# Four value-spread transfers started at separate points of a group, their mask in four instructions, and the key spread as one product

## The chip, the cores and the metric

One Trainium2 chip, and one of its cores. The metric is the device time of one launch in microseconds (us), of the slowest core; here there is only one. Five engines work beside each other: TensorE (matrix products; PE in the profile, PEld its weight loads), VectorE (DVE), ScalarE (ACT), GpSimd (POOL) and SyncE (SP), which starts most DMA transfers. They order their work by semaphores.

## The reference, cut to what matters

The program is a two-layer block: an attention layer, an expert layer (best two of eight), a second attention of another kind, an expert layer (best one), each followed by a sum and a layer norm. The change touches only the first attention. Its core, for 4096 tokens (16 sequences of 256), 128 channels in 16 heads of 8:

```
cs = cumsum(w, time);  cs_b = cs - w          # w: learned decay, per channel
A_f = (r * exp(cf)) @ (k * exp(-cf)).T        # cf, cb: cs and cs_b, shifted and clipped
A_b = (r * exp(-cb)) @ (k * exp(cb)).T
A   = where(i >= j, A_f, A_b)                 # per head, 256 x 256
y   = A @ v
```

Then y is normalized over each head, gated, projected, added to x and normalized; the rows go on to their experts.

## The kernel before, in words

`lion_stage` (from L130) computes this attention in eight groups n = 0 to 7 of 512 tokens. A head has only 8 channels, so TensorE works on four heads at once: keys are spread into a tile `kx` in which each of four copies keeps the channels of one head of four and holds zeros elsewhere, and values into a tile `vx`, of which likewise only the channels of a head are kept. Scores of one group are computed in eight parts m = 0 to 7 (`scores`, L432); each part's scores go from PSUM to SBUF by a ScalarE copy (L688), VectorE puts the other triangle in place (L895), and TensorE multiplies with the values (`attend`, L452), one part behind. Between these, each engine's `step(n)` does pieces of the projection work for group n+1 and of the closing work for group n-1, in an order written out by hand.

Scores of part m increase `s_sc` to 8n+m+1, so `s_sc >= 8(n-1)+5` says that part 4 of group n-1 is done.

The path of the values: in part 3 of group n-1 ScalarE writes the projected values of group n to `vt` (L643). SyncE (`spread_values`, L290) stores them in HBM (L294, 256 KB) and, when that has landed, reads them back in another order by four transfers, one for each 32 partitions of `vx` (L299, 256 KB each, all with the same source). GpSimd multiplies `vx` with the 0/1 matrix `vhead` (`mask_values`, L596, the instruction L600, 128x2048). `attend(n, 0)` waits for it, in part 1 of group n. SyncE's list continues with the residual rows (L315), the input of group n+3 (L273, after part 6 of group n) and the store of the finished rows (L303).

GpSimd's list in each group n: the scatter of group n-2's rows to the experts' regions (L573, eight indirect DMAs; not in groups 0 and 1), the mask for group n+1, the norm of group n-1 (L580 to L593). A scatter waits for VectorE's `dispatch` (L877) in part 3.

The keys: VectorE spreads one half (`spread`, L752; L755, four instructions of 128x256) of `kx` and ScalarE the other (L627), each in two halves of a group: half 0 for group n+1 in part 6, half 1 in part 3. After half 0 VectorE does, in part 7, the gate (L790) and the mix input of group n+2 (L763, L764, L765), for which TensorE waits in part 0 (L345).

Of the kernel before, what the change touches and what calls it, by code (L numbers as in the profile page):

```python
# [18 lines left out]
ALU = mybir.AluOpType  # L19
# [3 lines left out]
P = 128  # L23
# [3 lines left out]
GT = 4  # L27
GTOK = GT * P
# [101 lines left out]
def lion_stage(nc, sem, x_in, x_out, w, consts, route):  # L130
# [15 lines left out]
    with ctx:  # L146
        def sb(name, shape, dt=F32):
            return ctx.enter_context(nc.sbuf_tensor("a_" + name, shape, dt))
# [5 lines left out]
        C = {k: con[:, a:b] for k, (a, b) in where.items()}  # L154
# [27 lines left out]
        rk = [sb(f"rk{i}", [P, 4, GTOK]) for i in range(2)]  # L182

        kx = sb("kx", [P, 2, GTOK // 32, 4, 32])
        vx = [sb(f"vx{i}", [P, GTOK // 32, P]) for i in range(2)]
# [65 lines left out]
        s_vd, s_vxp, s_vx = [[sem(f"lion_v_{n}_{i}") for i in range(2)] for n in ("stored", "spread")] + [sem("lion_v_chunks")]  # L251
        s_kk, s_kd, s_ktp, s_kt = sem("lion_keys_scaled"), sem("lion_r_scaled"), sem("lion_keys_transposed"), sem("lion_key_rows")
        s_kx = sem("lion_keys_spread")
        s_stp, s_st = sem("lion_states"), sem("lion_states_masked")
        s_sc, s_ata, s_atd = sem("lion_scores"), sem("lion_scores_copied"), sem("lion_diagonals_masked")
# [14 lines left out]
        @block.sync  # L270
        def _(sp):
            one = lambda rows, n: rows[n]
            load_x = lambda n: sp.dma_start(xp[n % 2][:, :, 1:SEQ + 1], xT_rows[n]).then_inc(s_x[n % 2], 16)  # L273
            sp.wait_ge(s_zero, 4)
            load_x(0)
            loads = [(con[:], consts[:, columns]), (maa[:], w["maa"]), (maa_w1[:], w["maa_w1"]),
                     (dec_w1[:], w["dec_w1"]), (dec_w2[:], w["dec_w2"]), (decay[:], w["decay"]),
                     (wT[:], w["wT"]), (woe[:, 0:P], w["wT"][:, 4, :]), (lnwb[:], w["lnwb"]), (gw[:], route["gate_w"])]
            for dst, src in loads:
                sp.dma_start(dst, src).then_inc(s_w, 16)  # L280
            for f in range(NF):
                r = D_MIX * (f % 4)
                sp.dma_start(maa_w2[r:r + D_MIX, f // 4, :], w["maa_w2"][f]).then_inc(s_w, 16)
            load_x(1)
            for b in range(2):
                sp.dma_start(xr[b][:], x_rows[b]).then_inc(s_xr[b], 16)
            sp.wait_ge(s_padr, 1)
            sp.dma_start(route["regions"][DUMMY * P:DUMMY * P + P], pad[:]).then_inc(s_pads, 16)

            def spread_values(n):  # L290

                b = n % 2
                sp.wait_ge(s_vt, n + 1)
                sp.dma_start(v_rows[b], vt[:]).then_inc(s_vd[b], 16)  # L294
                if n >= 2:
                    sp.wait_ge(s_y, n - 1)
                sp.wait_ge(s_vd[b], 16 * (n // 2) + 16)
                for h in range(4):
                    sp.dma_start(vx[b][32 * h:32 * h + 32], v_chunks[b]).then_inc(s_vxp[b], 16)  # L299

            def store_rows(n):
                sp.wait_ge(s_xo, n + 1)
                sp.dma_start(o_rows[n], xo[n % 2][0][:, :, 0:P]).then_inc(s_out[n % 2], 16)  # L303

            spread_values(0)
            for n in range(NG):
                if n + 1 < NG:
                    spread_values(n + 1)
                if n == 0:
                    sp.wait_ge(s_xf, NF)  # L310
                    sp.wait_ge(s_xgp, 1)
                    load_x(2)
                if n and n + 1 < NG:
                    sp.wait_ge(s_z, n)
                    sp.dma_start(xr[(n + 1) % 2][:], x_rows[n + 1]).then_inc(s_xr[(n + 1) % 2], 16)  # L315
                if n + 3 < NG:
                    sp.wait_ge(s_sc, 8 * n + 7)
                    load_x(n + 3)
                if n:
                    store_rows(n - 1)  # L320
                if n == NG - 3:
                    for dst, src in route["weights"]:
                        sp.dma_start(dst, src).then_inc(s_mw, 16)
            store_rows(NG - 1)
            sp.wait_ge(s_tab, 1)
            for e in range(NE):
                end = sp.value_load(ends[0:1, e:e + 1], min_val=0, max_val=e * REGION + TOK)
                sp.dma_start(route["regions"][bass.ds(end, P), :], pad[:]).then_inc(s_pads, 16)
            for b in range(2):
                sp.wait_ge(s_out[b], 16 * (NG // 2))  # L330
            sp.wait_ge(s_mw, 16 * len(route["weights"]))
            sp.wait_ge(s_pads, 16 * (1 + NE))
# [216 lines left out]
        def _(pool):  # L549
# [46 lines left out]
            def mask_values(n):  # L596

                b = n % 2
                pool.wait_ge(s_vxp[b], 64 * (n // 2) + 64)
                nc.gpsimd.tensor_tensor(vx[b][:], vx[b][:], C["vhead"].unsqueeze(1).broadcast_to([P, GTOK // 32, P]),  # L600
                                        ALU.mult).then_inc(s_vx, 1)

            pool.wait_ge(s_w, NW)
            mask_values(0)
            for n in range(NG):
                if n >= 2:
                    scatter(n - 2)
                if n + 1 < NG:
                    mask_values(n + 1)
                if n:  # L610
                    norm(n - 1)
# [128 lines left out]
        def _(dve):  # L740
            v = nc.vector
# [9 lines left out]

            def spread(n, half):  # L752

                for h in range(4):
                    i = v.tensor_scalar(kx[:, 0, 8 * half:8 * half + 8, h, :],  # L755
                                        rk[n % 2][:, 1, half * 256:half * 256 + 256].rearrange("p (c j) -> p c j", j=32),
                                        C["heads4"][:, h:h + 1], None, ALU.mult)
                i.then_inc(s_kx, 1)

            def mix_input(k):  # L760
                b = k % 2
# [189 lines left out]
            scale_r(0)  # L951
            dve.wait_ge(s_kk, 1)
            spread(0, 0)
            gate(0)
            mix_input(1)
# [1746 lines left out]
```

## Time and profile before

| | us |
|---|---|
| three runs | 1222.15, 1222.37, 1225.36 (median 1222.37) |
| profiled execution, its own time | 1220.72 |
| its span | 1218.6 |
| TensorE busy (matmul) | 959.9 (79%) |
| VectorE busy | 749.2 (61%) |
| ScalarE busy | 554.4 (45%) |
| GpSimd busy | 487.4 (40%) |

The span reaches from the first to the last instruction of the profiled execution; 2.1 us lie around it. Matmul ends are modelled, so a busy TensorE isn't one at its peak. The stage with the change fills about the first 396 us. A row of the timeline gives start, duration, engine, line, operation, output tile and inputs, and shape, with how many instructions were merged; the bracket gives the idle time before it and what ended it. "issue" there means that nothing which the profile shows was waited for, and "remote" that the releaser wasn't identified.

### The profile page before, as it was taken

To read this page: it belongs to the slowest core of one execution; us is meant where nothing else is said; L and a number is where in the kernel's file an instruction comes from. 1 tells how busy PE (TensorE), PEld (TensorE's weight loads), DVE (VectorE), ACT (ScalarE), POOL (GpSimd) and SP (SyncE) were. 2 spreads that over 40 slices of the span, in tenths; PEclk is the share of its full clock that TensorE was granted. 3 is DMA by queue.
4 is the path that set the end of the run, shared out by engine and by line. 5 is a ranking of instruction groups with operands and counts; after the bars stand their busy time and mean duration, and the time that the engine had idled before them with its cause. 6 is when DMAs were issued, how large, how long until landed. Compare 5 with 4: busy or idle time off the path is not lost. (4 is left out here: it accounts for less than half of the span.)

```text
span 1218.6 us, 34137 instructions
## 1 busy us (share of the span) xinstructions
PE 959.9 (79%) x12733; PEld 678.2 (56%) x12734; DVE 749.2 (61%) x2236; ACT 554.4 (45%) x1120; POOL 487.4 (40%) x596
## 2 busy tenths in 40 slices
PE   5689898889871699995488858569999998525995
PEld 2456565556560688895244436466566664214885
DVE  3768786777544355553288875914887655742664
ACT  1365555456520355552266752144444444314664
POOL 0113334532546244443477620021164332533776
PEclk8798998898855799998699998867977666757998
DMA  3122321325201222220433331131111124002210
GB/s 92 37 63 70 74 54 51 89 71 175 71 29 52 59 56 58 58 56 25 115 87 88 62 87 65 70 89 61 47 54 54 54 60 160 18 13 54 56 53 22
DMA packets 122117, 79.50 MB, mean 65 GB/s; under 512 B 46979, under 2 KB 108521, under 8 KB 121600
## 3 DMA queue, kind: packets, MB, share of 16 engines
q1 hardware_dynamic: 115328, 64.95, 19.9%
q0 software_dynamic: 6656, 12.70, 3.3%
q8 instruction: 93, 1.52, 0.5%
q14 instruction: 40, 0.33, 0.1%
HBM read 49.05 MB, written 27.51 MB: 63 GB/s over the span
## 5 line engine op out<-in xcount | busy, mean ns | idle before, releaser
L1134 ACT ACTIVATE bx_h<-bx_up,bx_cur 128x128 f32<-128x128 f32 x288 | 82.1, 368 | 104.2 <-PE bx_up L1105 104.2
L573 POOL DMA_INDIRECT regions_b<-a_xo,a_seat x64 | 63.6, 994 | 149.7 <-DVE a_seat L877 132.6
L688 ACT ACTIVATE a_at<-a_scores 128x1024 f32<-128x1024 f32 x64 | 65.5, 1024 | 120.2 <-PE a_scores L447 89.9
L1063 POOL DMA_INDIRECT chosen_b<-bx_ys,bx_to x72 | 76.4, 1061 | 90.4 <-DVE bx_ys L1177 88.5
L442 PE MATMUL a_scores<-a_rk,a_kx 32*128 32x128 f32 (+3 forms) x1024 | 72.8, 317 | 27.3 <-issue 11.5
L442 PEld LDWEIGHTS a_scores<-a_rk,a_kx 32*128 32x128 f32 x1024 | 55.5, 210 | 55.6 <-issue 38.6
L1105 PE MATMUL bx_up<-bx_xT,bx_cur 128*128 128x128 f32 x576 | 82.8, 288 | 1.9 <-issue 0.5
L1087 PE MATMUL bx_down<-bk_w,bx_h 128*128 x576 | 82.0, 285 | 0.4 <-ACT bx_h L1134 0.4
L1105 PEld LDWEIGHTS bx_up<-bx_xT,bx_cur 128*128 128x128 f32 x576 | 71.4, 195 | 11.1 <-issue 5.3
L600 POOL TENSOR_TENSOR a_vx<-a_vx,a_con 128x2048 f32<-128x2048 f32 x8 | 36.2, 4525 | 99.0 <-DMA a_vx<-lion_values 99.0
L1087 PEld LDWEIGHTS bx_down<-bk_w,bx_h 128*128 128x128 f32 x576 | 69.8, 191 | 3.9 <-issue 0.6
L1331 PE MATMUL c_bank<-c_xT,c_wc 128*128 128x512 f32 x128 | 60.6, 616 | 11.1 <-ACT c_xT L1450 11.1
L1150 DVE TENSOR_SCALAR bx_cur<-bk_w 128x516 f32 x72 | 30.9, 429 | 58.5 <-issue 55.8
L447 PE MATMUL a_scores<-a_rk,a_kx 32*128 32x32 f32 (+3 forms) x1024 | 64.9, 301 | 0.9 <-issue 0.8
L2152 POOL COPY g_kak<-keep_k 128x512 f32<-128x512 f32 x16 | 13.6, 857 | 101.6 <-POOLq L2654 76.9
L447 PEld LDWEIGHTS a_scores<-a_rk,a_kx 32*128 32x128 f32 x1024 | 53.5, 216 | 1.0 <-issue 0.8
L1985 PE MATMUL g_hidden<-g_xT,g_g 128*128 128x512 f32 x64 | 49.2, 869 | 3.4 <-ACT g_hid L2287 3.4
L1402 POOL TENSOR_SCALAR c_xn<-c_part,c_mv,c_rsv 128x128 f32<-128x128 f32 x32 | 35.0, 1104 | 37.8 <-ACT c_rsv L1444 37.8
L1331 PEld LDWEIGHTS c_bank<-c_xT,c_wc 128*128 128x128 f32 x128 | 24.5, 196 | 45.2 <-issue 43.1
L2387 DVE TENSOR_TENSOR g_xyx<-g_eye,g_wu_xy 128x256 f32<-128x256 f32 x12 | 5.0, 421 | 71.7 <-PE g_wu_xy L1945 71.7
L895 DVE COPY_PREDICATED a_at<-a_earlier,a_scores 128x256 f32<-128x256 uint32 x64 | 28.1, 439 | 32.6 <-ACT a_at L688 31.6
L1105 PE MATMUL dx_up<-dx_xT,dx_cur 128*128 128x128 f32 x320 | 47.1, 291 | 0.7 <-ACT dx_cur L1123 0.2
(431 smaller groups left out, 2564.2 us busy)
## 6 DMA issues: line engine op xcount, KB each, us to landing
a_vx<-lion_values SPq DMA_DIRECT2D x32, 256.0 KB
bx_xs<-regions_b SPq DMA_DIRECT2D x72, 65.0 KB, 1.8
bk_w<-in_b_w SPq DMA_DIRECT2D x16, 256.0 KB, 5.9
c_part<-chosen_b SPq DMA_DIRECT2D x16, 256.0 KB, 3.9
space<-in_d_w SPq DMA_DIRECT2D x16, 256.0 KB
dx_xs<-regions_d SPq DMA_DIRECT2D x40, 65.0 KB, 1.8
a_xp<-in_a_xT SPq DMA_DIRECT2D x8, 256.0 KB, 3.4
a_xr<-in_x SPq DMA_DIRECT2D x8, 256.0 KB
```

The lines of the kernel that those rows point to most:

```text
L442: mm(S4[:, g, o:o + P - 32 * q], kx[rows, 0, 4 * t + q].rearrange("p h j -> p (h j)"), rk[b][rows, 0, t * P + 32 * q:(t + 1) * P], start=T ...
L447: i = mm(S4[:, g, o + P - 32 * q:o + P + 32], kx[rows, 1, 4 * t + q].rearrange("p h j -> p (h j)"), rk[b][rows, 2, t * P:t * P + 32 * q + 32],
L573: nc.gpsimd.indirect_dma_start(route["regions"], bass.IndirectOffsetOnAxis(ap=seat[b][:, k, t:t + 1], axis=0), xo[b][k][:, t, :], None).th ...
L600: nc.gpsimd.tensor_tensor(vx[b][:], vx[b][:], C["vhead"].unsqueeze(1).broadcast_to([P, GTOK // 32, P]), ALU.mult).then_inc(s_vx, 1)
L688: op(at[m % 2][:], S4[:, :, 0:320].rearrange("p g (q k) -> p g q k", q=2)[:, :, :, 0:P], ACT.Copy).then_inc(s_ata, 1)
L1063: nc.gpsimd.indirect_dma_start(dest, bass.IndirectOffsetOnAxis(ap=to[u][:, 0:1], axis=0), ys[u][:], None, bounds_check=dest.shape[0] - 1, ...
L1087: i = mm(BY[u % 2][:, 0:P], h[u % 2][:, f, :], w2[:, bass.ds(e, 1), f, :].rearrange("p e c -> p (e c)"), start=(f == 0), stop=(f == FC - 1))
L1105: i = mm(BU[u % 2][:, f * P:(f + 1) * P], cur[u % 2][:, f * P:(f + 1) * P], xT[u % 2][:], start=True, stop=True)
L1134: i = op(h[u % 2][:, f, :], BU[u % 2][:, f * P:(f + 1) * P], act_fn, bias=cur[u % 2][:, FC * P + f:FC * P + f + 1])
L1331: i = mm(B[1 + k].rearrange("p (s t) -> p s t", s=GSEQ), wc[:, k, j, :], xT[:, :, j:SEQ + j], start=(j == 0), stop=(j == 3))
L1402: nc.gpsimd.tensor_scalar(xn[:, t, :], part[b][0][:, t, :], mv[:, t, 0:1], rsv[:, t:t + 1], ALU.subtract, ALU.mult).then_inc(s_xn, 1)
L1985: mm(H[j % 2].rearrange("p (k h c) -> p k h c", h=4, c=32), g1[:], x.unsqueeze(2).broadcast_to([P, 4, 4, 32]), start=True, stop=False)
```

## The change

SyncE starts the first of the four transfers as before; the others wait until parts 4, 5 and 6 of the group before have their scores (from the second group on). GpSimd's mask is written as four instructions of 128x512, with the semaphore on the last. VectorE's half of the key spread is one product of 128x1024, with the keys and the 0/1 columns both broadcast, in place of four instructions that scale by a column. What is computed stays the same.

```diff
                 for h in range(4):
+                    if n and h:
+                        sp.wait_ge(s_sc, 8 * (n - 1) + 4 + h)
                     sp.dma_start(vx[b][32 * h:32 * h + 32], v_chunks[b]).then_inc(s_vxp[b], 16)
...
-                nc.gpsimd.tensor_tensor(vx[b][:], vx[b][:], C["vhead"].unsqueeze(1).broadcast_to([P, GTOK // 32, P]),
-                                        ALU.mult).then_inc(s_vx, 1)
+                for t in range(GT):
+                    i = nc.gpsimd.tensor_tensor(vx[b][:, 4 * t:4 * t + 4], vx[b][:, 4 * t:4 * t + 4],
+                                                C["vhead"].unsqueeze(1).broadcast_to([P, 4, P]), ALU.mult)
+                i.then_inc(s_vx, 1)
...
-                for h in range(4):
-                    i = v.tensor_scalar(kx[:, 0, 8 * half:8 * half + 8, h, :],
-                                        rk[n % 2][:, 1, half * 256:half * 256 + 256].rearrange("p (c j) -> p c j", j=32),
-                                        C["heads4"][:, h:h + 1], None, ALU.mult)
-                i.then_inc(s_kx, 1)
+                keys = rk[n % 2][:, 1, half * 256:half * 256 + 256].rearrange("p (c j) -> p c j", j=32)
+                v.tensor_tensor(kx[:, 0, 8 * half:8 * half + 8], keys.unsqueeze(2).broadcast_to([P, 8, 4, 32]),
+                                C["heads4"].unsqueeze(1).unsqueeze(3).broadcast_to([P, 8, 4, 32]), ALU.mult).then_inc(s_kx, 1)
```

## Rows read from the trace of the kernel before

**Rows 1.** The page's first line: span and instructions.
```profile
span 1218.6 us, 34137 instructions
```

**Rows 2.** Stretches (length; busy PE, PEld, DVE, ACT, POOL; clock; DMA; GB/s).
```profile
187.00:228.00 41.00, 36.21 (x557) 23.93 (x556) 29.68 (x91) 22.26 (x32) 17.43 (x17) 0.92 0.25 66
...
188.00:190.00 2.00, 1.03 (x3) 0.85 (x3) 0.00 (x0) 0.00 (x0) 1.98 (x2) 0.50 0.66 195
...
289.00:291.00 2.00, 2.00 (x28) 0.97 (x22) 0.77 (x3) 1.97 (x3) 0.00 (x0) 1.00 1.03 366
```

**Rows 3.** ScalarE's timeline: copies of part 6, group 1; parts 5, 6, group 3.
```profile
109.35 1.02 ACT L688 ACTIVATE a_at<-a_scores 128x1024 f32<-128x1024 f32 x1 [1.08 <-PE a_scores L447]
...
183.13 1.02 ACT L688 ACTIVATE a_at<-a_scores 128x1024 f32<-128x1024 f32 x1 [4.21 <-remote]
...
192.29 1.02 ACT L688 ACTIVATE a_at<-a_scores 128x1024 f32<-128x1024 f32 x1 [6.25 <-PE a_scores L447]
```

**Rows 4.** TensorE's timeline, part 6 of group 3 and part 0 of group 4.
```profile
188.84 2.02 PE L442 MATMUL a_scores<-a_rk,a_kx 32*128 32x128 f32 x5 [0.95 <-issue]
...
200.85 1.12 PE L345 MATMUL a_free<-a_xin,a_maa_w 128*128 128x512 f32 x2 [0.22 <-DVE a_xin L765]
```

**Rows 5.** GpSimd's timeline: first scatter, mask, norm, copy of rows, group 3.
```profile
178.84 1.12 POOL L573 DMA_INDIRECT regions_b<-a_xo,a_seat  x1 [19.66 <-DVE a_seat L877]
...
188.81 4.54 POOL L600 TENSOR_TENSOR a_vx<-a_vx,a_con 128x2048 f32<-128x2048 f32 x1
...
193.65 1.04 POOL L583 TENSOR_TENSOR a_rsv<-a_vr,a_power 128x4 f32<-128x4 f32 x1
...
198.13 0.61 POOL L593 COPY a_xo<-a_xo 128x512 f32<-128x512 f32 x1
```

**Rows 6.** Timeline of group 7: scores of part 5, their copy, scores of part 6.
```profile
345.22 0.79 PE L447 MATMUL a_scores<-a_rk,a_kx 32*128 32x128 f32 x8
...
347.88 1.02 ACT L688 ACTIVATE a_at<-a_scores 128x1024 f32<-128x1024 f32 x1 [5.94 <-remote]
...
353.58 0.58 PE L442 MATMUL a_scores<-a_rk,a_kx 32*128 32x96 f32 x4 [0.89 <-issue]
```

**Rows 7.** SyncE's timeline, group 3: store, four spread transfers, residual load.
```profile
175.77 0.37 SPq L294 DMA_DIRECT2D lion_values<-a_vt  x1
178.12 2.05 SPq L299 DMA_DIRECT2D a_vx<-lion_values  x4
186.91 0.39 SPq L315 DMA_DIRECT2D a_xr<-in_x  x1
```

**Rows 8.** VectorE's timeline: mix input without overlap, then from the key spread, group 3.
```profile
78.51 0.68 DVE L763 TENSOR_TENSOR a_nb<-a_xp 128x512 f32<-128x512 f32 x1
...
195.10 1.21 DVE L755 TENSOR_SCALAR a_kx<-a_rk,a_con 128x256 f32<-128x256 f32 x4
197.33 0.45 DVE L895 COPY_PREDICATED a_at<-a_earlier,a_scores 128x256 f32<-128x256 uint32 x1 [1.02 <-ACT a_at L688]
...
198.43 0.86 DVE L763 TENSOR_TENSOR a_nb<-a_xp 128x512 f32<-128x512 f32 x1
...
201.65 0.18 DVE L843 TENSOR_TENSOR a_lg<-a_mv,a_gsum 128x32 f32<-128x32 f32 x1
```

**Rows 9.** Timeline: key spreads that a mask overlaps (start-up, groups 0, 1).
```profile
37.58 5.41 DVE L755 TENSOR_SCALAR a_kx<-a_rk,a_con 128x256 f32<-128x256 f32 x4
38.09 4.49 POOL L600 TENSOR_TENSOR a_vx<-a_vx,a_con 128x2048 f32<-128x2048 f32 x1 [36.48 <-DMA a_vx<-lion_values]
...
43.14 0.81 PE L442 MATMUL a_scores<-a_rk,a_kx 32*128 32x128 f32 x8 [5.50 <-DVE a_kx L755]
...
73.65 4.01 DVE L755 TENSOR_SCALAR a_kx<-a_rk,a_con 128x256 f32<-128x256 f32 x4
...
112.17 2.89 DVE L755 TENSOR_SCALAR a_kx<-a_rk,a_con 128x256 f32<-128x256 f32 x4
```

**Rows 10.** Grouped instructions of the stretch 0 to 400 us: the key spread.
```profile
L755 DVE TENSOR_SCALAR a_kx<-a_rk,a_con 128x256 f32<-128x256 f32 x64 | 27.8, 494 | 0.0
```

## The prediction

> **What bounds the kernel now.** The change lies in the first of five stages, so I read that stage alone; of the profile's page I use only the span [rows 1], since its chain of waits follows the last stage. The stage runs eight groups of 512 tokens, each in parts 0 to 7. First view: busy times by stretch. In one group period of 41 us TensorE is busy 36.2, VectorE 29.7, GpSimd 17.4 [rows 2]: TensorE leads, and what makes it wait costs whole time. Second view: ScalarE's timeline. Its copy of part 5's scores comes at 183.13 and of part 6's at 192.29, 9.2 us apart, the latter after a wait of 6.25 for TensorE [rows 3]. TensorE in turn shows one or two matmuls at a time with gaps that no wait explains ("issue") [rows 4], busy 1.03 of 2 us, and the granted clock falls to 0.50, the 1.2 GHz level [rows 2]. This stall recurs in groups 2 to 6. It lies over GpSimd's eight indirect DMAs (the scatter, 178.84 to 188.8) [rows 5].
>
> Is it the spread's burst (four transfers begun within 2.05 us from 178.12 [rows 7]) or the scatter? Three readings speak. Group 1 has the burst and no scatter: there the copy of part 6 waits only 1.08 us [rows 3]. Group 7 has a scatter and no burst: ScalarE's copy of part 5 still starts at 347.88, though the scores it reads ended at 346.0, and TensorE shows the same "issue" gaps until 353.58 [rows 6]. And while weights stream in at 366 GB/s TensorE is busy 2.00 of 2 us [rows 2]. So the scatter makes most of the stall. From these rows the stall of a middle group is about 7.4 us (2.6 on ScalarE, 183.13 less 180.5 where the scores ended by the pattern of group 7; 4.8 on TensorE), that of group 7 4.6 (1.9, and 2.7 of gaps): at most 2.8 us can belong to burst and other transfers.
>
> **The change, part by part.** All sums are against the profiled execution, 1220.7 us (span 1218.6 and 2.1 around it); the median of the runs is 1.7 above it, so I add the sum to 1222.4.
>
> (1) Three extra waits on SyncE. The spread for group n+1 is begun in part 4 of group n, after its store: store at 175.77, spread at 178.12 [rows 7]. Transfer 1 waits for part 4's scores (done at 176.6): nothing changes. Transfer 2 waits for part 5's, done about 180.5, so it moves by 1.4 us, and only transfer 3 really moves, to the end of part 6's scores: 192.3. So three of the four still run under the scatter. Behind that wait on SyncE stand the load of the residual (now 186.91 [rows 7]), the next input load and the store of rows. The first is used more than a group later, the second by a mix step a group later, the third is waited for two groups later: all hidden, and cost would begin only beyond some 30 us of lateness. What it relieves: the last transfer and the residual load no longer run beside the scatter. Bounds per group: 0, and the 2.0 us by which the copy of part 6 (192.29) lies after the stall's end at about 190.3 [rows 3, 4]; I take 0.5, nearer to 0, since group 7 stalls with neither, for the four groups 3 to 6: -2.0 us.
>
> (2) The mask comes later. It needs all four landed. Before, it starts at 188.81, directly behind the scatter [rows 5], and ends at 193.3, where VectorE has nothing to do. Now the last transfer starts at 192.35; the store of the same 256 KB takes 2.35 us from issue to the next step [rows 7], so the mask starts near 194.8 and, 4.5 us long, runs under VectorE's spread of keys (195.10) and mix input (198.43 to 200.8) [rows 8]. What the trace shows of the two beside each other: a key spread in the old form takes 5.41, 4.01 and 2.89 us where a mask overlaps it, 1.21 where none does [rows 8, 9]. For an operation with two inputs in SBUF there is one sort of row: L763 takes 0.86 us when a GpSimd copy from 198.13 to 198.74 overlaps its start, 0.68 when none does [rows 5, 8]: it waited almost until the copy's end.
>
> The Trainium skill says the same on the page "SBUF — State Buffer", section "Who interferes with whom": a VectorE instruction with two SBUF inputs contends with a GpSimd instruction that reads SBUF, and whichever starts first blocks the other for its whole length. It speaks against the new form of the key spread as an escape from the port. The trace agrees as far as the 0.86 against 0.68 goes; by the rule with whole pieces of 1.13 us the two waits worked out below would come to +2.1 us a group in place of 1.5, and without any contention to 0.
>
> With the mask in four instructions a piece takes 4.53/4 = 1.13 us, and one waits up to 1.0, typically 0.85 of it. Order in a middle group: piece 1 from 194.85; the key spread waits 0.75 (hidden: VectorE is idle 1.02 us before its next step, at 197.33 [rows 8]); piece 2 after it; piece 3 ahead of L763; piece 4 between L763 and L764. Two waits of 0.85, less the 0.2 which L763 loses already: +1.5 us. It is on the path, for TensorE waits 0.22 us for exactly this mix input at 200.85 [rows 4]. Bounds: 0 (VectorE always wins, or no contention) and 3.0 (three waits of 1.0). Group 6 has no mix input after it, so groups 2 to 5 pay: +6.0.
>
> Queued behind the mask on GpSimd: the norm's small operations (193.65, 1.04 us [rows 5]) move from 193.3 to about 201; VectorE reads their result at 201.65 [rows 8], itself moved to 203: hidden by about 1 us. Scatter and dispatch come 15 us later, and TensorE needs the masked values only about 10 us after the mask.
>
> (3) Three places where the old long mask blocks a key spread. Start-up: 5.41 instead of 1.2 us, and TensorE waits 5.50 us for it until 43.14 [rows 9]. Now the spread (37.58) is issued ahead of the mask (38.09) and runs free: 4.2 us gained, less two piece waits (1.7) in the mix input which TensorE wants next: -2.5, bounds -4.2 and 0. Group 0: 4.01-1.21 = 2.8 gained, 0.9 for a piece that the key spread waits for and 1.7 in the mix input lost: -0.2. Group 1: 2.89-1.21 = 1.7 gained, 2.6 lost: +0.9. Bounds for each of these two: the gain alone, and the loss with three full waits.
>
> (4) One product in place of four. Operations of this kind take 0.18 us for 32 columns and 0.68 for 512 [rows 8], so 1.05 ns a column and 1.22 us for 1024, against a mean of 4 x 0.344 that in fact overlap to 1.14: +0.09 us each. (The mean of 494 ns in the grouped row contains the blocked ones [rows 10].) Sixteen of them; the eight of part 6 lie in the 1.02 us of slack, those of part 3 are waited for by TensorE: 8 x 0.09 = +0.7. Bounds -0.5 and +3.
>
> Four mask instructions instead of one add perhaps 0.1 us each on GpSimd, inside the hidden part.
>
> Sum: -2.0 +6.0 -2.5 -0.2 +0.9 +0.7 = +2.9. Forecast: 1222.4+2.9 = **1225.3 us**, own range 1219 to 1230: a small loss that a measurement (0.3%, 3.7 us) hardly separates from none.
>
> **Rivals.**
> A, the mix input isn't held up: VectorE wins each tie, or isn't held by the pieces at all. Then part 2 is 0, start-up gives -4.2, groups 0 and 1 -2.8 and -1.7, part 4 +0.7, relief -2: -10, 1212. For it: ties of a few tenths decide. Against: the 0.86.
> B, the burst is the stall's main cause. Spacing takes half of 7.4 us in five groups (-18) while the mask still costs +5: 1209; if all of it goes, 1190. For it: burst and scatter begin within 1 us of each other. Against: group 7, and the burst is three quarters unmoved.
> C, slower: the later mask meets VectorE in full. Mechanism: each of the mix input's three operations waits a whole piece (3.0 in groups 2 to 5, 12 us), and the norm, a further 2 us late on GpSimd, makes VectorE's expert choice wait 0.5 us five times (2.5); start-up gains only 1.4, groups 0 and 1 lose 3, part 4 0.7, no relief: +17, 1239; with half of this 1231. It decides once the last transfer lands over 2.5 us after part 6, so that more pieces lie behind 198.4.
> That the waits change nothing (all met when reached) holds for the first of them, and is excluded for the third, since SyncE is there 12 us before part 6 ends.
>
> **How the numbers follow.** Forecast 0.45, A 0.22, B 0.08, C 0.25. Range 1209 to 1236: it takes in A, B's half, and C to above its half; what is left out is B's full case and C's full price, under 2 in 10. Within 0.3% means 1218.7 to 1226.0. Of the forecast's 0.45, 0.27 lies within and 0.18 above; A gives 0.20 faster, 0.02 same; B 0.08 faster; C 0.23 slower, 0.02 same. Faster 0.28, same 0.31, slower 0.41.
>
> **What would show it.** In the new profile: SyncE's fourth issue right behind part 6's scores; the mask's first piece 2.4 us later, and pieces with VectorE's L763 to L765 operations between them, each with a longer duration (about 1.5) than now; the "issue" gaps of TensorE still there in groups 2 to 6 until the scatter ends; start-up's key spread at 1.2 us and TensorE's first scores near 39. I am wrong if the gaps shrink by more than 2 us a group (B), if L763 to L765 keep 0.7 us beside a mask piece (A), or if the mask's end delays the norm past VectorE's choice (C).

## The result, and the profile after

The changed kernel takes 1241.93 us (median; 1238.38 to 1251.3), the kernel before in the same comparison 1223.86: a ratio of 1.0129, 95% interval 1.0081 to 1.0176. So it is slower, by 16 us at this ratio where 2.9 were forecast, and outside the range. The page's first line answers to [rows 1]:
```profile
span 1241.8 us, 34113 instructions
```
The span is 23.2 us longer. The first stage ends (first load of the next stage) at 421.73 us in place of 401.77: 20.0 of these lie in it, and 2.3 of these had passed before any changed instruction ran (the first store, 31.05 against 28.78).

First view, ScalarE's timeline of the changed kernel: the copies of the scores, which mark each part. The lines are those of [rows 3] (part 6 of group 1; parts 5 and 6 of group 3), with part 7 of group 3 and parts 0 and 1 of group 4 behind them.
```profile
114.14 1.02 ACT L692 ACTIVATE a_at<-a_scores 128x1024 f32<-128x1024 f32 x1 [1.08 <-PE a_scores L449]
...
194.08 1.02 ACT L692 ACTIVATE a_at<-a_scores 128x1024 f32<-128x1024 f32 x1 [4.20 <-remote]
...
203.02 1.02 ACT L692 ACTIVATE a_at<-a_scores 128x1024 f32<-128x1024 f32 x1 [6.03 <-PE a_scores L449]
...
207.23 1.02 ACT L692 ACTIVATE a_at<-a_scores 128x1024 f32<-128x1024 f32 x1 [1.59 <-PE a_scores L449]
...
209.97 1.02 ACT L692 ACTIVATE a_at<-a_scores 128x1024 f32<-128x1024 f32 x1 [0.60 <-PE a_scores L449]
...
216.99 1.02 ACT L692 ACTIVATE a_at<-a_scores 128x1024 f32<-128x1024 f32 x1
```
From part 5 to part 6 are 8.94 us, 9.16 before [rows 3]: the stall is untouched. From part 0 to part 1 are 7.02, where the kernel before has 5.10:
```profile
199.02 1.02 ACT L688 ACTIVATE a_at<-a_scores 128x1024 f32<-128x1024 f32 x1 [0.59 <-PE a_scores L447]
...
204.12 1.02 ACT L688 ACTIVATE a_at<-a_scores 128x1024 f32<-128x1024 f32 x1
```
This last step is longer in each group but the last: by 3.0, 3.0 and 3.3 us at start-up and in groups 1 and 2, by 1.5 to 2.2 in groups 3 to 6, in sum 16.7 us. (Steps are named by the group whose scores are copied; the prediction's middle "groups 2 to 5" begin the masks of groups 3 to 6.)

Second view, the timelines of SyncE, GpSimd, VectorE and TensorE in the same place; they answer to [rows 7], [rows 5], [rows 8] and [rows 4].
```profile
189.00 14.32 SPq L301 DMA_DIRECT2D a_vx<-lion_values  x4
...
206.10 6.23 POOL L603 TENSOR_TENSOR a_vx<-a_vx,a_con 128x512 f32<-128x512 f32 x4 [6.33 <-DMA a_vx<-lion_values]
...
209.38 1.83 DVE L765 TENSOR_TENSOR a_nb<-a_xp 128x512 f32<-128x512 f32 x1
...
211.24 1.64 DVE L766 SCALAR_TENSOR_TENSOR a_dx<-a_nb,a_xp 128x512 f32<-128x512 f32 x1
...
212.91 0.75 DVE L767 SCALAR_TENSOR_TENSOR a_xin<-a_dx,a_maa,a_xp 128x512 f32<-128x512 f32 x1
...
213.72 0.70 PE L347 MATMUL a_free<-a_xin,a_maa_w 128*128 128x512 f32 x1 [2.13 <-DVE a_xin L767]
```
The four issues now span 14.32 us in place of 2.05; the mask begins 2.8 us after the last one's issue is done (203.3), 6.3 us after GpSimd was free for it. Its four pieces take 6.23 us in place of 4.53, because VectorE's operations come between them; L765 and L766 take 1.83 and 1.64 us in place of 0.86 and about 0.7, and TensorE waits 2.13 us for the mix input, 0.22 before.

Third view, a stretch of 2 us under the scatter, which answers to the second line of [rows 2].
```profile
198.00:200.00 2.00, 0.85 (x4) 0.50 (x4) 0.00 (x0) 0.00 (x0) 1.46 (x2) 0.81 0.10 33
```
Four matmuls in 2 us, VectorE and ScalarE idle, as before; DMA is busy 0.10 of this stretch where it was 0.66 before. With hardly a transfer beside it the stall goes on, though three of the four transfers still ran under its beginning.

### The profile page after: what moved, and what is told of

It reads as the page before. It is cut to its first block and busy times, and to the rows that moved or that the text cites. A ratio compares the mean times of both kernels' runs of the same rounds, so it can differ in the third digit from the quotient of the medians.

```text
span 1241.8 us, 34113 instructions
## 1 busy us (share of the span) xinstructions
PE 985.9 (79%) x12733; PEld 688.0 (55%) x12734; DVE 758.9 (61%) x2188; ACT 554.4 (45%) x1120; POOL 504.5 (41%) x620
## 5 line engine op out<-in xcount | busy, mean ns | idle before, releaser
L603 POOL TENSOR_TENSOR a_vx<-a_vx,a_con 128x512 f32<-128x512 f32 x32 | 48.3, 1538 | 135.6 <-DMA a_vx<-lion_values 135.6
L444 PE MATMUL a_scores<-a_rk,a_kx 32*128 32x128 f32 (+3 forms) x1024 | 73.2, 321 | 19.1 <-issue 11.2
L1333 PE MATMUL c_bank<-c_xT,c_wc 128*128 128x512 f32 x128 | 63.6, 643 | 9.2 <-ACT c_xT L1452 9.1
```

Source lines behind the costliest of these rows:

```text
L444: mm(S4[:, g, o:o + P - 32 * q], kx[rows, 0, 4 * t + q].rearrange("p h j -> p (h j)"), rk[b][rows, 0, t * P + 32 * q:(t + 1) * P], start=T ...
L603: i = nc.gpsimd.tensor_tensor(vx[b][:, 4 * t:4 * t + 4], vx[b][:, 4 * t:4 * t + 4], C["vhead"].unsqueeze(1).broadcast_to([P, 4, P]), ALU.mult)
L1333: i = mm(B[1 + k].rearrange("p (s t) -> p s t", s=GSEQ), wc[:, k, j, :], xT[:, :, j:SEQ + j], start=(j == 0), stop=(j == 3))
```

## The experiments

The runs were made on five chips, and that turned out to matter, so each group names its chip. "The waits" are the change's on SyncE, "four pieces" its mask, "one product" its key spread. All ratios are against the kernel before on the same chip.

**Chip 1, the kernel before at 1224.6 us: the change taken apart.** My first theory was that the waits bring the late mask, and with it the whole loss; the rival, that the new key spread or the pieces cost by themselves.

The waits alone:
```
 for h in range(4):
+    if n and h:
+        sp.wait_ge(s_sc, 8 * (n - 1) + 4 + h)
```


> The kernel before with the three added waits of the transfers alone; mask and key spread as before. Theory (the late mask under VectorE's work is the price): the 4.5 us mask now starts near the key spread of part 6, which waits for nearly all of it, 3 to 4 us less the 1 us of slack in each of groups 1 to 6, so slower by 12 to 20 us. Rival 1 (the other two edits make the loss): no slower than 2 us. Rival 2 (the spacing relieves TensorE's gaps under the scatter): gaps shrink by over 2 us a group.

Measured 1.0162 (1.0115 to 1.0210). The waits alone lose all of it, as much as the whole change within the intervals. VectorE and GpSimd, group 3:
```profile
207.06 5.39 DVE L757 TENSOR_SCALAR a_kx<-a_rk,a_con 128x256 f32<-128x256 f32 x4
...
207.69 4.61 POOL L602 TENSOR_TENSOR a_vx<-a_vx,a_con 128x2048 f32<-128x2048 f32 x1 [6.81 <-DMA a_vx<-lion_values]
```
Late, the long mask meets the key spread (5.39 us in place of 1.21 [rows 8]), and the mix input begins 6.24 us after the key spread does (213.30), 3.33 before [rows 8].

The mask in four instructions alone:
```
-nc.gpsimd.tensor_tensor(vx[b][:], vx[b][:], ...)
+for t in range(GT):
+    i = nc.gpsimd.tensor_tensor(vx[b][:, 4 * t:4 * t + 4], ...)
```


> The kernel before with the mask in four instructions alone. Theory: in groups 2 to 6 the mask stays where VectorE is idle, so nothing; in start-up and groups 0 and 1 a key spread of four instructions waits for pieces and not for a whole mask, but mix input meets the rest: between -4 and +1 us. Rival (four pieces cost by themselves): slower by over 3 us.

Measured 1.0009 (0.9973 to 1.0044): nothing.

One product alone (the diff's last part):
```
-for h in range(4):
-    i = v.tensor_scalar(kx[:, 0, 8 * half:8 * half + 8, h, :], ...)
+v.tensor_tensor(kx[:, 0, 8 * half:8 * half + 8], keys..., heads4..., ALU.mult)
```


> The kernel before with the key spread as one product alone. Theory: 0.09 us longer at 8 places on the path and still blocked by the long mask in start-up and groups 0 and 1: between -1 and +2 us. Rival (the product is what costs): slower by over 4 us.

Measured 1.0019 (0.9981 to 1.0057). The start-up shows why there is no gain:
```profile
37.90 1.21 DVE L755 TENSOR_TENSOR a_kx<-a_rk,a_con 128x1024 f32<-128x1024 f32 x1
...
38.13 5.36 POOL L600 TENSOR_TENSOR a_vx<-a_vx,a_con 128x2048 f32<-128x2048 f32 x1 [36.52 <-DMA a_vx<-lion_values]
...
39.64 4.41 DVE L761 TENSOR_TENSOR a_nb<-a_xp 128x512 f32<-128x512 f32 x1
...
45.62 2.07 PE L345 MATMUL a_free<-a_xin,a_maa_w 128*128 128x512 f32 x2 [2.37 <-DVE a_xin L763]
```
The key spread, begun 0.23 us ahead of the mask, takes 1.21 us in place of 5.41 [rows 9], and now it is the mask that takes longer (5.36 us for 4.49). The mix input's first operation waits instead (4.41 for 0.68). The wait is moved on. Not every operation of VectorE waits: between the two the gate (L788), which reads one of its inputs from PSUM, starts at 39.04 under the mask and takes its usual 0.69 us.

Four pieces and one product, without the waits:

> Both of these, without the waits. Theory: the whole loss of the change hangs on the waits, so this is within -4 and +2 us of the kernel before. Rival: it keeps a third or more of the 16 us loss.

Measured 0.9986 (0.9945 to 1.0026). With waits_only it shows that on this chip the loss hangs on the waits.

**Chip 0, the kernel before at 1215.7 us: when the mask runs.**

Four pieces, one product, no waits on SyncE, but GpSimd waits until VectorE has scaled the queries in part 6, the step just ahead of the key spread, which was meant to start the mask as late as the change does:
```
+if n:
+    pool.wait_ge(s_kd, n + 1)
 for t in range(GT):
```


> The changed kernel without the waits on the transfers; in their place GpSimd itself waits, before each mask from group 1 on, until VectorE has scaled part 6's queries (about when the last transfer lands in the changed kernel). Theory (the mask's place is the price, however it comes there): as slow as the changed kernel, 1.0 to 1.6% above the kernel before. Rival (the transfers' own spacing or their meeting with other loads is the price): within 0.4% of the kernel before.

Measured 0.9908 (0.9874 to 0.9942): faster, against my theory. But the theory was hardly tried: only the masks begun in groups 0 and 1 were held back by the new wait; from group 2 on it was met when GpSimd reached it, and the mask began directly behind the scatter (in group 3 the scatter's last DMA ends at 190.70, the mask begins at 190.72).

The changed kernel, the mask held back until the mix input is done:
```
+if n + 1 < NG:
+    pool.wait_ge(s_xin, n + 2)
```


> The changed kernel, with GpSimd waiting before each mask until VectorE's mix input has been written, so that the two no longer run side by side. The mask comes 2 to 3 us later still. Theory (contention with the mix input is the price): its three operations take 0.7 us each and the kernel gains 6 to 14 us on the changed one, unless the norm behind the mask is then late for VectorE's choice of experts (up to 2 us a group given back). Rival (lateness itself is the price): slower than the changed kernel.

Measured 0.9975 (0.9953 to 0.9996). The changed kernel itself didn't run on this chip; why holding the mask back gains so little is shown by the repeat on chip 3, below.

The changed kernel, its last transfer begun with the third, at the scores of part 5:
```
-sp.wait_ge(s_sc, 8 * (n - 1) + 4 + h)
+sp.wait_ge(s_sc, 8 * (n - 1) + (5, 6, 6)[h - 1])
```


> The changed kernel with the last transfer waiting for part 5's scores in place of part 6's, so that it lands while the scatter still runs. Theory: the mask is back behind the scatter in groups 2 to 6 and the loss is gone but for groups 0 and 1: within 0.4% of the kernel before. Rival (any spacing costs): slower by over 0.7%.

Measured 0.9874 (0.9837 to 0.9912).

The kernel before, the spread of groups 2 to 7 cut to a sixteenth:
```
-sp.dma_start(vx[b][32 * h:32 * h + 32], v_chunks[b])
+sp.dma_start(vx[b][32 * h:32 * h + 32, 0:1], v_chunks[b][:, 0:1])
```


> The kernel before, but from group 2 on each of the four transfers moves one sixteenth of its data (the values of these groups are left stale): what the burst itself costs. Theory (the scatter makes the gaps of TensorE, not the burst): gaps under the scatter stay, at most 2 us a group shorter, so 0 to 8 us faster. Rival (the burst makes them): the copy of part 6 follows that of part 5 by 4 us in place of 9.2, and the kernel is over 20 us faster.

Measured 0.9992 (0.9959 to 1.0024). All four profiles surprised me in one thing: part 4 to 5 takes 3.88 us and 5 to 6 some 4.8 in groups 3 to 6, together 8.7, where each profile so far had about 6.5 and 9, together 15.2 to 15.7. The stall was gone from kernels that share no edit. Either each takes it away by its own doing, or it hangs on the chip.

**Chip 6, the kernel before at 1229.6 us: two of them again, beside both kernels.**

> The kernel before, unchanged, profiled once more. Open is why the four last profiles (mask_late_by_wait, mask_after_mix, last_at_part5, small_spread) show no stall under the scatter: their copies of the scores of part 5 and part 6 start 3.9 and 4.8 us after the copy ahead of them, where every earlier profile has 6.5 and 9.1. Theory S: the stall is a state of the chip or of the execution, and no edit took it away. Then this profile can show either pattern, and it shows the one that the other three profiles of this call show; without the stall the scatter ends before the group does, and the long mask meets the key spread, so that from the copy of part 7 to that of part 0 there are about 8.2 us in place of 2.7, group period about 40, and the span stays within 10 us of 1218. Theory T: each of the four edits takes the stall away by its own doing. Then this profile shows 6.5 and 9.1 again (period 41), whatever the others show.

> The changed kernel, unchanged, profiled once more beside before_again. Theory S: it has or lacks the stall as before_again does. With the stall the ratio is 1.013 again (1.008 to 1.018). Without it, the last transfer waits for the scores of part 6, which now come 7 us earlier, the mask still runs under the mix input (part 0 to part 1 about 9.4 us), but the key spread is no longer held: period about 37.5 to 38.5 against 40, so a ratio of about 0.985 to 0.995: the sign of the change would turn with the stall. Theory T: ratio 1.013 and steps of 6.5 and 9.1.

> last_at_part5 once more (the changed kernel, its last transfer begun at the scores of part 5 as the third is). Theory S: it shows the stall if before_again does, and then costs about 1.005 to 1.013 of before, like the changed kernel; without the stall 0.987 again. Theory T: no stall (3.9 and 4.8 us) and 0.987 in either case, while before_again has the stall.

> mask_late_by_wait once more (the kernel before, GpSimd waiting for VectorE's key spread of part 6 ahead of the mask; nothing of the change). Theory S: as before_again: with the stall about 1.01 (the one long mask under the mix input, what the late mask costs by itself), without it 0.991 again. Theory T: no stall and 0.991 whatever before_again shows.

(The text on record errs in one point: mask_late_by_wait holds the four pieces and the one product too, as shown above; it lacks only the waits on SyncE.) All four profiles have the stall: together 15.7 to 15.8 us in groups 3 to 6. Ratios: before_again 1.0005 (0.9968 to 1.0043), after_again 1.0078 (1.0043 to 1.0114), last_again 1.0005 (0.9962 to 1.0049), mask_late_again 1.0127 (1.0083 to 1.0171). The same two kernels that gained 0.9 and 1.3% on chip 0 lose 1.3% or gain nothing here. The stall belongs to the chip, not to an edit. (Each chip appears in one group of runs only, so chip and hour can't be told apart.)

mask_late_again is also the run that shows the cause. It has no wait on SyncE; here GpSimd's own wait does hold the mask back, by 6.61 us in group 3,
```profile
201.64 6.24 POOL L603 TENSOR_TENSOR a_vx<-a_vx,a_con 128x512 f32<-128x512 f32 x4 [6.61 <-DVE a_rk L804]
```
and it loses at least as much as the change beside it (three executions). last_again, whose mask begins directly behind the scatter (186.79 in group 3), loses nothing. So the lateness of the mask is the price, and not the spacing of the transfers.

**Chip 3, the kernel before at 1214.7 us.**

The changed kernel with `range(GT)` of the mask's loop cut to `range(1)`:

> The changed kernel with only the first of the four mask instructions (three quarters of the spread values stay unmasked). Transfers and waits stay those of the change. Theory M: the loss is the late mask beside VectorE's mix input and key spreads. Then L765 and L766 of the mix input fall from 1.8 and 1.6 to 0.7 us, the step from part 0 to part 1 from 6.9 to about 5, and the ratio from 1.008 to 1.013 down to 0.990 to 0.998 (the four-piece mask with the one product and no waits gave 0.9986 with the pieces still there). Theory Q: the three waits cost by themselves, through what is queued behind them on SyncE or through later transfers. Then the ratio stays at 1.005 or above though the mix input is short.

Measured 0.9611 (0.9547 to 0.9676), the stage ending at 347.9 us. VectorE and TensorE, group 3 to 4:
```profile
172.69 0.70 DVE L765 TENSOR_TENSOR a_nb<-a_xp 128x512 f32<-128x512 f32 x1
...
173.43 0.69 DVE L766 SCALAR_TENSOR_TENSOR a_dx<-a_nb,a_xp 128x512 f32<-128x512 f32 x1
...
174.15 0.75 DVE L767 SCALAR_TENSOR_TENSOR a_xin<-a_dx,a_maa,a_xp 128x512 f32<-128x512 f32 x1
...
174.96 1.12 PE L347 MATMUL a_free<-a_xin,a_maa_w 128*128 128x512 f32 x2
```
With all three waits in place, each operation is back at its undisturbed time and TensorE waits for nothing. The gain is larger than theory M gave (0.990 to 0.998), which was worked out for a chip with the stall; it also leaves out three quarters of the mask's own time on GpSimd. Theory Q finds no support, but this chip could hardly show it, for here the waits hold the mask back by 0.43 us at most from group 2 on; what speaks against Q is mask_late_again.

Two repeats, wanted on a chip with the stall; this one has none, so they only repeat chip 0:

> mask_after_mix once more (the changed kernel, GpSimd waiting for the mix input ahead of the mask), wanted on a chip that shows the stall. Theory M as a pure port cost: the step from part 0 to part 1 is back to about 5 us and the ratio near 0.998. Theory M with the queue: the norm is queued behind the mask on GpSimd, so VectorE's expert choice (L847) waits about 5 us for a_rsv, the step from part 1 to part 2 grows from 4.7 to about 10, and the ratio is 1.01 or more with the stall, against 0.9975 on the chip without it.

> small_spread once more (the kernel before, the spread of groups 2 to 7 cut to a sixteenth of its bytes, old values kept), wanted on a chip that shows the stall. If the spread's burst makes half of the stall or more (rival B of the prediction), the steps part 4 to 5 and 5 to 6 fall below 5.2 and 7.0 us and the ratio below 0.99. If the burst has no part in it, they stay at 6.5 and 9.1 and the ratio is 0.997 to 1.003. If this chip has no stall at all, before_again on another chip doesn't tell, and the ratio is 0.999 as it was.

Measured 1.0000 (0.9970 to 1.0029) and 0.9979 (0.9947 to 1.0010). Both kernels of small_spread leave most of the values out. Whether that would shorten the stall on a chip that has it stays untried. mask_after_mix_again shows what queues behind a held mask (GpSimd, then VectorE's expert choice):
```profile
199.89 4.93 POOL L605 TENSOR_TENSOR a_vx<-a_vx,a_con 128x512 f32<-128x512 f32 x4 [4.67 <-DVE a_xin L769]
...
205.12 1.05 POOL L585 TENSOR_TENSOR a_rsv<-a_vr,a_power 128x4 f32<-128x4 f32 x1
...
206.20 0.19 DVE L847 TENSOR_TENSOR a_lg<-a_mv,a_gsum 128x32 f32<-128x32 f32 x1 [5.53 <-POOL a_rsv L585]
```
The mix input is free (0.68, 0.69, 0.75 us) and the norm pays: the step from part 1 to 2 is 10.5 us in place of 4.7.

The kernel before with GpSimd's order turned:
```
-scatter(n - 2); mask_values(n + 1); norm(n - 1)
+mask_values(n + 1); norm(n - 1); scatter(n - 2)
```


> The kernel before with another order on GpSimd: mask, norm, and only then the scatter of the group before. If the scatter's eight indirect DMAs bring the stall, it leaves parts 4 to 6 (steps 3.9 and 4.8 us in groups 2 to 6) and stands where the scatter now runs, under parts 0 to 3 of the next group, with TensorE's one matmul at a time there. If it belongs to those parts of the program and not to the scatter, the steps stay at 6.5 and 9.1. On a chip without the stall neither is seen.

Measured 0.9887 (0.9810 to 0.9963). No stall on this chip, so it doesn't say whether the stall would follow the scatter.

**Chip 8, the kernel before at 1215.0 us: both kernels without the stall.**

> The kernel before, unchanged. Profiles of two chips (the kernel before at 1225 to 1230 us there) show the stall in parts 4 to 6 in each kernel, those of two others (the kernel before at 1215) in none, but none of the latter is of the kernel before itself. Theory S: if this chip has no stall, this profile shows steps of 3.9 and 4.8 us, and about 8.2 us from part 7 to part 0 with a key spread (L757) of 4 to 5 us beside the mask, like small_spread's, and the time is 1211 to 1218. If it has the stall: 6.5, 9.1 and 2.7 us and 1222 to 1230. Against S: steps of 6.5 and 9.1 and a time near 1215.

> The changed kernel, unchanged. Theory S without the stall: steps of 3.9 and 4.8 us, part 7 to 0 at 2.75, part 0 to 1 at 9.4 us as in last_at_part5, ratio 0.985 to 0.992, so the change is a gain there. With the stall: 1.008 to 1.013, as twice before.

Measured 0.9989 (0.9964 to 1.0014) and 0.9935 (0.9908 to 0.9963). The kernel before, ScalarE's copies of parts 5, 6, 7 of group 3 and 0 and 1 of group 4, then VectorE and GpSimd:
```profile
185.86 1.02 ACT L688 ACTIVATE a_at<-a_scores 128x1024 f32<-128x1024 f32 x1 [1.57 <-PE a_scores L447]
...
190.65 1.02 ACT L688 ACTIVATE a_at<-a_scores 128x1024 f32<-128x1024 f32 x1 [0.94 <-PE a_scores L447]
...
193.67 1.03 ACT L688 ACTIVATE a_at<-a_scores 128x1024 f32<-128x1024 f32 x1 [0.41 <-PE a_scores L447]
...
201.85 1.02 ACT L688 ACTIVATE a_at<-a_scores 128x1024 f32<-128x1024 f32 x1 [6.03 <-PE a_scores L447]
...
207.57 1.02 ACT L688 ACTIVATE a_at<-a_scores 128x1024 f32<-128x1024 f32 x1
```
```profile
193.47 5.93 DVE L755 TENSOR_SCALAR a_kx<-a_rk,a_con 128x256 f32<-128x256 f32 x4
```
```profile
194.19 4.52 POOL L600 TENSOR_TENSOR a_vx<-a_vx,a_con 128x2048 f32<-128x2048 f32 x1
```
The group reaches part 7 9.5 us after the scatter's start (184.21), 17.4 with the stall, but the mask still stands behind the scatter on GpSimd, and so it now falls on the key spread (5.93 us): part 7 to 0 takes 8.18 us in place of 2.74. That is why the stall, 7.0 us (15.7 less 8.7) in each of groups 3 to 6 alone, costs this kernel only 10 to 15 us in all (1225 to 1230 against 1215). The stall used to cover the mask.

The changed kernel there, ScalarE's copies of part 7 of group 3 and parts 0 and 1 of group 4, then VectorE, GpSimd and TensorE:
```profile
191.11 1.03 ACT L692 ACTIVATE a_at<-a_scores 128x1024 f32<-128x1024 f32 x1 [0.40 <-PE a_scores L449]
...
193.85 1.02 ACT L692 ACTIVATE a_at<-a_scores 128x1024 f32<-128x1024 f32 x1 [0.59 <-PE a_scores L449]
...
203.13 1.02 ACT L692 ACTIVATE a_at<-a_scores 128x1024 f32<-128x1024 f32 x1
```
```profile
190.91 1.21 DVE L759 TENSOR_TENSOR a_kx<-a_rk,a_con 128x1024 f32<-128x1024 f32 x1
...
191.64 6.20 POOL L603 TENSOR_TENSOR a_vx<-a_vx,a_con 128x512 f32<-128x512 f32 x4
...
193.26 1.78 DVE L765 TENSOR_TENSOR a_nb<-a_xp 128x512 f32<-128x512 f32 x1
...
195.07 1.64 DVE L766 SCALAR_TENSOR_TENSOR a_dx<-a_nb,a_xp 128x512 f32<-128x512 f32 x1
...
196.75 1.63 DVE L767 SCALAR_TENSOR_TENSOR a_xin<-a_dx,a_maa,a_xp 128x512 f32<-128x512 f32 x1
...
198.44 2.07 PE L347 MATMUL a_free<-a_xin,a_maa_w 128*128 128x512 f32 x2 [2.97 <-DVE a_xin L767]
```
and its stretches of 2 us (columns as in [rows 2]):
```profile
196.00:198.00 2.00, 0.00 (x0) 0.00 (x0) 1.97 (x2) 0.00 (x0) 2.00 (x3) 1.00 0.02 4
198.00:200.00 2.00, 1.56 (x2) 0.50 (x2) 1.64 (x5) 0.00 (x0) 1.81 (x3) 0.51 0.00 0
200.00:202.00 2.00, 2.00 (x7) 0.29 (x7) 1.83 (x17) 0.00 (x1) 2.00 (x3) 0.64 0.00 0
```
The key spread runs free, all three operations of the mix input wait for a piece, TensorE is idle for the 2 us before 198 and then gets 0.51 and 0.64 of its clock: L347's two matmuls take 2.07 us where they take 1.12 at full clock [rows 4]. Part 0 to 1 takes 9.28 us against 5.72 in before_third (+3.6), part 7 to 0 2.74 against 8.18 (-5.4): the change gains. Over groups 1 to 7 of the two profiles the steps from part 7 to 0 take 33.9 us less in sum, those from 0 to 1 17.6 more and those from 1 to 2 11.2 more; not every group gains (group 6 loses 3.9 us from part 1 to 2, where TensorE runs at 0.50 of its clock from 275 to 289).

The waits have hardly a part in this. In group 3 both kernels begin the mask directly behind the scatter, 10.0 us after the scatter's start (194.19 less 184.21, 191.64 less 181.65): without the stall the scatter ends when the last transfer has landed; only the masks begun in groups 4 and 6 waited for it, 0.52 and 1.25 us. So on this chip the other two edits act, and of them the one product is ahead of the mask by 0.7 us and gets through. Which of the two gains wasn't tried apart on such a chip. With the stall, part 6's scores come so late that the waits do hold the mask back (6.33 us in group 3), and before the change there is no held key spread in groups 3 to 6 to be freed (1.21 us [rows 8]); there only the loss in the mix input is left.

## Why the prediction was wrong, point by point

In short: the late mask, the stall untouched and the wait moved on to the mix input were right, and the sums were too small. Of the 14.8 us between the 2.9 forecast and the 17.7 that the stage lost behind its start, some 7 lie in terms that were there: the relief of (1), which did not come, and above all the mix input's wait in (2) and (3), counted as two pieces where three operations waited at start-up and in groups 1 and 2. The other 8, nearly, had no term at all; most of it stands in steps in which TensorE ran at 0.50 of its clock.

What bounds the kernel: right. VectorE's and TensorE's chain through key spread and mix input set each group, and TensorE's wait for the mix input was where the change struck.

(1) Relief: -2.0 forecast, 0 measured. The last transfer and the residual load left the stall's stretch, and the step was 8.94 against 9.16; on chip 6, group 4, 9.16 against 9.17. The relief that rival B hoped for did not come: with the last transfer and the load gone from it the stall stays, and on chip 8 it is absent with the whole burst in place. Whether the burst has a part in the stall where there is one stays open. The reading "the scatter makes most of the stall" was an inference from groups 1 and 7 of one chip. It isn't shown: in before_third the same scatter runs under the same burst at a DMA share of up to 1.21 with TensorE busy 2.00 of 2 us.

(2) The late mask: right in kind, a little small. The mask began 2.8 to 3.9 us after the last issue was done (groups 2 to 6), not 2.4, past the point from which rival C was to decide. In groups 3 to 6 two operations of the mix input waited, as forecast; the one that began in step with a piece took 0.8 to 1.15 us more, not 0.85, the one that met a piece under way 0.3 to 0.6. Forecast +6.0 for the masks of groups 3 to 6; their steps grew by 1.5, 1.9, 1.8 and 2.15: +7.4. By itself that was within bounds. It isn't a constant: in the pair of chip 6 the same steps grew by -0.5, 1.7, 0.8 and 0.0, +2.1 in sum. In group 6 there TensorE still worked at a low clock at the end of the group (part 7 to 0 4.54 us) and wanted the mix input only after it was ready (part 0 to 1 4.61 us in both kernels).

(3) Start-up and the first two groups failed more. Start-up: the first scores came 2.8 us earlier relative to the store (4.2 forecast); the mask began ahead of the key spread here (40.15 and 40.80), and the product took 1.69 us and not 1.2, so the order that was forecast turned. The mix input behind them took back 3.0 (1.7 forecast): about 0, not -2.5. (On chip 6 these two are -3.0 and +2.0, on chip 8 -3.5 and -0.2: one pair of profiles doesn't fix them.) The mask begun in group 0: -2.9 and +3.0 (the steps into and in group 1), near the -0.2 that was forecast. Group 1's: -1.6 and +3.3, +1.7 for +0.9. Each time all three operations waited (at start-up 1.16, 1.64 and 1.63 us for 0.68, 0.69 and 0.75). The Trainium skill's page "SBUF — State Buffer", section "Who interferes with whom", has whichever instruction starts first block the other for its length. Here the trace of after_third agrees: of a 6.20-us mask and three operations at 1.78, 1.64 and 1.63 us, the pieces and the operations take turns, 1.13 us for a piece and some 0.55 for an operation between two ((6.20 less 4.53)/3). But the turn isn't sure: in group 2 of the same profile the first operation waited for all four pieces, and the other two ran free:
```profile
151.32 4.95 POOL L603 TENSOR_TENSOR a_vx<-a_vx,a_con 128x512 f32<-128x512 f32 x4
...
151.62 5.22 DVE L765 TENSOR_TENSOR a_nb<-a_xp 128x512 f32<-128x512 f32 x1
```
The same comes in that group of mask_late_by_wait and of last_at_part5 (5.21 us both). Why the turn fails there is open.

(4) One product: its duration was right (1.22 us forecast, 1.21 to 1.22 measured but at start-up), its effect by itself not measurable (1.0019).

What had no term in the sum: with 10 us so far (0 + 7.4 + 0 + 0.1 + 1.7 + 0.7, the first numbers of each part, (4) as forecast), some 8 of the 17.7 us behind the start are left. The steps from part 7 to part 0 of groups 3, 5 and 7 took 1.95, 1.96 and 1.1 us more, of group 6 1.8 less; parts 6 to 7 1.7 more in sum, parts 2 to 4 of group 0 2.2 more. TensorE runs there at 0.50 of its clock for longer: before part 0 of group 5 from 252 to 256, where the kernel before has 1.00 at the same place of group 3 (195 to 197), and in group 0 from 60 to 66. Kernels without the change show such steps as well (4.70 us in before_again, part 0 of group 5; 4.55 in the kernel before, group 6), so part of this is the execution and not the change, and how much is open: for the same kernel 1.0129 and 1.0078 were measured on two chips.

The rivals: C came nearest (1239 against 1241.9), but by its number more than by its terms. Its first half, 12 us for three whole waits in the middle groups, measured 7.4, with two waits. Its second half (the norm late, the choice waiting) was 0.3 us in two groups of the changed kernel, in after_third 0.3 in three groups, 1.57 in group 5 and 2.83 in group 7, and 5.5 in each middle group only in mask_after_mix. What made up the difference is what had no term. A was wrong for the mix input. No rival said that the sign depends on the chip, and that was the main thing to be learned: 1.3 and 0.8% slower on two chips with the stall, 0.65% faster on one without. This follows from a premise of the prediction that held only on chips with the stall: that the mask directly behind the scatter falls where VectorE has nothing to do.

A better version: the last transfer begun at the scores of part 5 is 0.9874 without the stall (chip 0; the change 0.9935 on chip 8) and 1.0005 with it (the change 1.0078 beside it on chip 6). It stands ahead of the change on chip 6, by intervals that just overlap (0.9962 to 1.0049, 1.0043 to 1.0114), and beats the kernel before only where the stall is absent. There scatter_last does as well (0.9887, chip 3), by the order on GpSimd alone.

## What to carry to other kernels

When a GpSimd pass over SBUF is to be moved, ask first what VectorE does at its new time: cutting it into pieces doesn't end the wait, it deals it out, as a rule one piece to each VectorE operation that reads its inputs from SBUF, and if those lead to TensorE the path pays all of them. Taking away one blocked operation hands the wait to the next one in line; only less work of GpSimd beside it removes it (three quarters of the mask left out: 0.961, the change itself 0.9935, both on chips without the stall). And read a stall that no wait explains on a second chip before building on it: here it decided the sign.

## What the hardware showed that was not expected

- A stall of TensorE, VectorE and ScalarE together, idle time named "issue" or "remote", in parts 4 to 6 of groups 2 to 6 and in group 7, in all profiles of two chips (and of the chip of the first comparison) and in none of three others, with the same programs. The scatter itself takes 10.0 us with the stall and without (178.84 to 188.81, 184.21 to 194.19). What brings it is open; scatter_last and small_spread were meant to tell and ran only where it is absent.
- A mask of 4.5 us in one instruction holds up a key spread or a mix-input operation that begins under it until it ends (5.93, 5.39, 4.41 us), though not one that reads an input from PSUM (0.69 us under the mask). The hold goes the other way too: a mask begun 0.23 us after the product takes 5.36 us.
- A late input can cost more than the wait. Behind TensorE's idle 2.97 us in group 4 of after_third the granted clock is 0.51 and 0.64 for 4 us, and the pair of 512-column matmuls takes 2.07 us against 1.12. Behind its 2.13 us in the changed kernel (first comparison, group 4) the clock stays at 1.00 and the pair takes 1.13.
